# Row sums of the first layer's softmax: from VectorE's reductions to ScalarE's accumulated output

## The reference, cut to what is computed

```python
# x, ctx: 16 x 128 x 128, float32; 16 heads of 64
x = x + L0_xattn(keys=ctx, queries=layernorm(x), values=ctx)   # causal mask
x = x + L0_ffn(layernorm(x))         # width 352, inputs and weights quantised to blockwise FP4
x = x + L1_xattn(layernorm(x), ctx)  # two softmaxes: 77 text keys, 51 image keys, summed
x = x + L1_ffn(layernorm(x))         # 8 experts, top 2
# attention of the first layer
scores = q @ k.T / 8, masked to the lower triangle
attn = softmax(scores, axis=-1)      # exp(scores - row max) / row sum
out  = (attn @ v) @ Wo
```

## Time and profile before

| | us |
|---|---|
| median of 3 runs | 676.44 (675.97 to 677.09) |
| the profiled execution | 680.06 |
| its span, first to last instruction | 678.3 |
| first layer's attention, by the mask additions and the second layer's first maximum | 12.1 to 257.2 |
| busy: TensorE, VectorE, ScalarE, GpSimd | 619.6, 531.7, 440.1, 309.9 |

### The profile page before, as it was taken

The page is one execution under the profiler, slowest core; times in us unless marked ns, Lnnn a source line. Parts: engine busy times, 40 slices in busy tenths (PEclk is TensorE's granted clock), DMA queues, the critical chain, the costliest instruction groups (busy, mean ns, idle before and its releaser), DMA issues.

```text
span 678.3 us, 16643 instructions
## 1 busy us (share of the span) xinstructions
PE 619.6 (91%) x5833; PEld 569.8 (84%) x5833; DVE 531.7 (78%) x1446; ACT 440.1 (65%) x1125; POOL 309.9 (46%) x444
## 2 busy tenths in 40 slices
PE   5897999999999899999999999999999978989980
PEld 5786889988888799999989989889889967989980
DVE  5788897898988989888898896888565585656645
ACT  6776789887778786556665655565655364556750
POOL 3565344444444344454444442435245664466550
PEclk9899999999999999999999999999998898989995
DMA  9700000000000000336553050000000001112215
GB/s 225 247 2 1 1 2 1 2 1 2 1 1 1 3 17 1 126 88 140 102 121 83 2 156 1 2 1 2 2 13 21 28 29 49 54 53 69 75 48 190
DMA packets 49610, 33.34 MB, mean 49 GB/s; under 512 B 9508, under 2 KB 46088, under 8 KB 49528
## 3 DMA queue, kind: packets, MB, share of 16 engines
q1 hardware_dynamic: 47256, 27.61, 16.4%
q0 software_dynamic: 2272, 4.67, 2.1%
HBM read 17.64 MB, written 14.63 MB: 48 GB/s over the span
## 4 chain that ended last, share of the span: by engine, by line
PE 54%; issue 15%; DVE 15%; POOL 10%; ACT 4%; DMA 1%; another core or an unknown queue 0%; POOLq 0%; SPq 0%; DVEq 0%; ACTq 0%
PE ps_j L587 7%; PE ps_s L756 6%; PE ph L1705 5%; PE ps_h L809 5%; POOL probs L1521 5%; PE ps_t L794 5%; PE py L1716 4%; PE ps_h L826 4%; PE ps_j L367 4%; PE ps_j L369 3%; PE ps_j L368 3%; POOL xs_scratch L1632 3%; DVE scores L1246 3%; DVE neg_max L1253 2%; DVE sums L1261 2%
## 5 line engine op out<-in xcount | busy, mean ns | idle before, releaser
L1521 POOL TENSOR_TENSOR probs<-scores,rsums 128x308 f32<-128x308 f32 (+1 forms) x192 | 153.9, 816 | 215.2 <-DVE rsums L1266 213.4
L1261 DVE TENSOR_REDUCE sums<-scores 128x4 f32<-128x308 f32 (+1 forms) x192 | 90.7, 500 | 20.1 <-ACT scores L983 14.4
L953 ACT ACTIVATE probsT<-ps_t 128x512 f32<-128x512 f32 x128 | 76.1, 594 | 30.7 <-PE ps_t L794 29.8
L794 PE MATMUL ps_t<-ident,probs 128*128 128x128 f32 x512 | 79.8, 279 | 9.2 <-POOL probs L1521 8.5
L983 ACT ACTIVATE scores<-scores,neg_max 128x128 f32<-128x128 f32 x256 | 81.4, 393 | 1.7 <-DVE neg_max L1253 1.6
L756 PE MATMUL ps_s<-KT,QT 64*128 64x128 f32 x1024 | 75.3, 287 | 0.8 <-ACT KT L856 0.8
L809 PE MATMUL ps_h<-probsT,V 128*64 128x128 f32 x1024 | 70.9, 281 | 4.7 <-DVE x_sb L1026 4.7
L850 ACT ACTIVATE QT<-ps_j 128x512 f32<-128x512 f32 x64 | 38.3, 598 | 56.4 <-PE ps_j L369 56.0
L794 PEld LDWEIGHTS ps_t<-ident,probs 128*128 128x128 f32 x512 | 59.5, 142 | 13.5 <-POOL probs L1521 12.3
L756 PEld LDWEIGHTS ps_s<-KT,QT 64*128 64x128 f32 x1024 | 63.0, 189 | 8.9 <-issue 2.6
L826 PE MATMUL ps_h<-Wo,headsT 128*128 128x128 f32 x512 | 69.6, 280 | 1.0 <-ACT headsT L946 1.0
(11 more groups left out here) (238 smaller groups left out, 1615.8 us busy)
## 6 DMA issues: line engine op xcount, KB each, us to landing
xs_scratch<-xs SPq DMA_DIRECT2D x8, 1032.0 KB, 7.3
xt<-xs_scratch SPq DMA_DIRECT2D x39, 64.5 KB
w1b<-in_L_ffn_w_dram SPq DMA_DIRECT2D x1, 2048.0 KB, 8.2
big_raw<-in_L_ffn_w_dram SPq DMA_DIRECT2D x8, 256.0 KB, 4.5
ysum<-y_scratch SPq DMA_DIRECT2D x4, 512.0 KB, 5.3
Wo<-in_L_xattn_Wo_dram SPq DMA_DIRECT2D x2, 512.0 KB, 5.0
out_dram<-x_sb SPq DMA_DIRECT2D x4, 256.0 KB, 2.3
x_sb<-in_x_dram SPq DMA_DIRECT2D x3, 256.0 KB, 10.3
```

What stands on the lines that cost most here:

```text
L794: ins = nc.tensor.transpose(ps_pT[:, j * S:(j + 1) * S], probs[s % 2][:, j, :], ident[:, :])
L953: nc.scalar.activation(probsT[(s - 2) % 4][:, :, :].rearrange("p h s -> p (h s)"), ps_pT[:, :], ACT.Copy).then_inc(SS["pT_copied"], 1)
L1261: ins = nc.vector.tensor_reduce(sums[:, p4, i, :], scores[p4][:, :, k0:k1], AX_X, ALU.add)
L1521: ins = nc.gpsimd.tensor_tensor(probs[(s - 1) % 2][:, :, k0:k1], scores[r][:, :, k0:k1], rsums[:, r, i, :].rearrange("p (h a) -> p h a", a ...
```

## The change

ScalarE's four exponentials of a step in the first layer get an accumulated output: each writes the sum of its row into `sums`, the tile that VectorE's reduction wrote before. `exp_sums` returns at once for the first layer. `invert_sums` of the first layer waits for `exp_ready` in its place. The second layer is as before, but for `sum_ready`, which now counts from its first step. The trace shows an accumulated output of L864 as an instruction of its own, ACTIVATION_READ_ACCUMULATOR, behind the ACTIVATE.

```diff
--- before.py
+++ after.py
@@ -981,7 +981,8 @@
                         act.wait_ge(SS["max_ready"], n + 1)
                         for j in range(HB):
                             ins = nc.scalar.activation(scores[s % 4][:, j, :], scores[s % 4][:, j, :], ACT.Exp,
-                                                       bias=neg_max[:, s % 4, 0, j:j + 1])
+                                                       bias=neg_max[:, s % 4, 0, j:j + 1],
+                                                       accum_out=sums[:, s % 4, 0, j:j + 1])
                     else:
                         act.wait_ge(SS["shifted"], g * STEPS + s + 1)
                         ins = nc.scalar.activation(scores[s % 4][:, :, :], scores[s % 4][:, :, :], ACT.Exp)
@@ -1256,13 +1257,18 @@
 
             def exp_sums(n, p4, lay):
 
+                if lay == 0:
+                    return
                 dve.wait_ge(SS["exp_ready"], n)
                 for i, (k0, k1) in enumerate(SEGS[lay]):
                     ins = nc.vector.tensor_reduce(sums[:, p4, i, :], scores[p4][:, :, k0:k1], AX_X, ALU.add)
                 ins.then_inc(SS["sum_ready"], 1)
 
             def invert_sums(n, p4, lay):
-                dve.wait_ge(SS["sum_ready"], n)
+                if lay == 0:
+                    dve.wait_ge(SS["exp_ready"], n)
+                else:
+                    dve.wait_ge(SS["sum_ready"], n - GROUPS * STEPS)
                 nc.vector.reciprocal(rsums[:, p4, 0:len(SEGS[lay]), :],
                                      sums[:, p4, 0:len(SEGS[lay]), :]).then_inc(SS["sums_ready"], 1)
```

## The result

The changed kernel takes 668.12 us (median of 4 runs, 667.17 to 670.2), the kernel before 676.21 us beside it. The ratio is 0.9887, with a 95% interval from 0.9861 to 0.9913, so 8.1 us faster. The forecast was 666.7 with a range from 661.0 to 675.0. The profiled execution took 667.7 us, its span is 665.9.

A forecast was written before the change was run, and what follows sets the result against it. TensorE's instruction stream was taken to set the pace, with waits from VectorE's lateness on top. Terms -1.0 - 4.0 - 5.7 + 1.0 = -9.7 us, off the 676.44 us median, gave 666.7 us, range 661.0 to 675.0.

The forecast's parts named there:

- What bounds the kernel: First layer: TensorE's own instruction stream sets the pace, and waits caused by VectorE being late come on top.
- The price of a read: ScalarE, first layer: each of 256 accumulator reads costs 0.095 us, bounds 0 and 0.19, 24 us in all.
- 12.1 to 54: First layer's opening stretch in us: a little over half of TensorE's 1.8 us wait for probs goes, -1.0 us.
- the rounds: Three repeating ten-step stretches of 39.8 us, each with one FFN round: -1.9 us each, -5.7 in all.
- Rival C: First layer: TensorE's busy time hides room and ScalarE's occupancy sets the time; -24.6 us, 651.8 us, chance 0.05.
- 40 x 0.095 = 3.8 gives 35.6 of 39.9: One ten-step round: 40 exponentials' reads add 3.8 us to ScalarE, which is then busy 35.6 of 39.9 us.
- 98 to 137.7: First-layer stretch in us: nothing to win, ScalarE rises to 39.4 of 39.7 busy; +1.0 us, bounds 0 and +2.5.
- Rival A: First layer: later exponentials delay ScalarE's copies, TensorE waits for QT, KT or headsT; -3.8 us, 672.6 us, chance 0.18.
- The moved wait: VectorE's 14.4 us wait for exponentials moves from the sum to the reciprocal; costed at nothing, at most 0.38 a step.
- The signs: Expected in the new profile: VectorE 38 to 43 us less busy, ScalarE 24 more, silu_h and x_sb waits gone.
- rival B: First layer: ScalarE becomes the pace if a read costs 0.19 us; about +7 us, 683.7 us, chance 0.09.
- Rival D: Whole kernel: nothing measurable, the waits were TensorE's pipeline draining anyway; within 1.4 us of 676.44, chance 0.07.

The follow-up runs named there:

- the kernel with no sum: Against the kernel before: no row sum in the first layer, neither VectorE's reductions nor ScalarE's reads, reciprocal of a constant; 657.95 us, ratio 0.9743.
- the changed kernel's second trace: The changed kernel run and traced again without alteration, against the kernel before: 667.0 us, ratio 0.9866, first layer 238.5 us.
- before, sum later: The kernel before, with VectorE's sum in even steps of the first layer moved behind the x_sb update and first mask addition; 682.11 us, ratio 1.0032.
- the sums on both engines: The kernel before plus accumulated outputs on the exponentials, written to an unread spare tile, VectorE's reductions kept; 692.0 us, ratio 1.0235.
- even steps only: Against the kernel before: accumulated sums only in the first layer's even steps, VectorE still summing in odd steps; 675.8 us, ratio 0.9995.

## Why the prediction's total was right, and where its terms were not

The total fell where it was forecast, at 668.1 against 666.7. Its terms did not. Here they are beside the traces, as changes of the first layer's stages against the kernel before. The gain is that of the kernel with no sum. The cost is the changed kernel's second trace minus that one. The last column is the changed kernel in its first and second trace. The gain and the last column hold in steps 0 to 21 up to 1.5 us of the clock that the kernel before lost there. With the same VectorE work but a clock of 1.00 (before, sum later) steps 0 to 11 took 46.4 us, against 47.3.

| stage | forecast | gain | cost of reads | changed |
|---|---|---|---|---|
| steps 0 to 21 | -5.0 | -10.1 | +4.2 | -7.1, -5.9 |
| 22 to 33 | +1.0 | -0.3 | +1.8 | +1.5, +1.5 |
| 34 to 43 | -1.9 | -2.1 | +2.0 | 0.0, 0.0 |
| 44 to 53 | -1.9 | -3.0 | +1.9 | -1.1, -1.1 |
| 54 to 63 | -1.9 | -2.4 | +1.3 | -1.1, -1.1 |
| sum | -9.7 | -17.8 | +11.2 | -7.8, -6.6 |

**What bounds the kernel** was right. TensorE's stream sets the pace, VectorE's lateness lay on top, and without it TensorE hardly idles.

**The price of a read** was right. I took 0.095 us by the squares' rows, and the four exponentials grew from 1.17 to 1.54 us, 0.093 each. The exponentials' line alone was busy for 81.38 us of the first layer before, and is for 105.04 now, 23.7 more. ScalarE's busy time rose by only 16.4. I read that as more overlap of neighbours. Its copies run closer together now (185.87 to 186.35, 0.48 us, for an instruction of 0.59), and in the first layer it waits 23.1 us for TensorE, where it waited 39.2 before.

**The gain was too small by 7 us,** in two terms. For 12.1 to 54 I took 1.0 of the waits named for probs. No sum at all gave 5.0 up to step 11 and 5.1 from step 12 to 21. And in the rounds I counted the idle time that the waits name, 2.4 us at most. The kernel with no sum suggests that TensorE's busy time held waits too. In the first layer its busy time fell from 227.3 to 222.9 us with the same matmuls. So 13.4 of the 17.8 us were idle time, and 4.4 were shown as busy. I take these for waits too. Some can be the clock lost before, though the later sum, with 1.00 in the whole layer, was as busy (227.4). This bears on the rule of the Trainium skill that I weighed (Perfetto Trace Analysis, section Identifying the Most-Contended Engine). The section warns that matmul busy time is not a good measure of the distance to the limit. Here it hid 4.4 us of room. Weight loads, busy for 36.0 of 39.5 us in a stretch in which TensorE was never idle, show 3.5 us of room in that stretch alone, and no run here won it. Rival C, which went by it, is out: with the reads gone too, the time was 658, not 652.

**The cost was too small by 8 to 10 us.** The step that failed is "40 x 0.095 = 3.8 gives 35.6 of 39.9" taken as free room. I charged the reads only in 98 to 137.7, where ScalarE was nearly full. They cost 1.3 to 2.0 us a round all the same. Part of it shows as waits. With no sum TensorE waited 1.2 us for ScalarE's copies in the first layer, in the changed kernel's second trace 6.0, and 3.5 of the new 4.8 are for probsT. Another 5.1 us of the 11.2 lie in TensorE's busy time (222.9 to 228.0), where the profile names no wait. Here an engine that stands in the chain of every step cost time before it was full. Rival A described this in kind: the new waits for ScalarE's copies passed the 4 us that I gave as its sign, with 6.3, though most are for probsT and A named QT, KT and headsT. By that sign the forecast was wrong in its mechanism though its number held. Rival A stood at -3.8 in size, because it had the small gain as its base. The two errors, 7 us and 8 to 10, have opposite signs and nearly cancel. That the total came within 1.4 us is luck.

**The moved wait,** costed at nothing, gave a gain of 3.5 us of the first layer against the same wait at the old place. My reason for calling it free did not hold as such. I had half a microsecond left ahead of the reciprocal. In the changed kernel VectorE waits there, as its timeline shows:

```profile
184.87 0.69 DVE L1247 TENSOR_TENSOR scores<-ps_s,causal 128x512 f32<-128x512 f32 x1
186.01 0.18 DVE L1272 RECIPROCAL rsums<-sums 128x4 f32<-128x4 f32 x1 [0.45 <-ACT scores L983]
186.10 0.68 DVE L1247 TENSOR_TENSOR scores<-ps_s,causal 128x512 f32<-128x512 f32 x1
```

Relieved of its sums, VectorE gets there before ScalarE does. In the profile it waited 20.2 us at the reciprocal in all, where it had waited 14.4 at the sum. The shorter chain of a step (the reciprocal 0.30 us earlier) has no term of its own in the sum either. The two together were worth 8.7 us of the medians while the reductions' time stayed on VectorE; what part of that is clock isn't known.

**The signs.** VectorE is 38.1 us less busy, as forecast. The waits for silu_h and x_sb shrank to a third and did not vanish. Those for probs went. ScalarE is 16.4 us busier, not 24. The rounds took 39.8, 38.7 and 38.7 us, not 37.9. The stretch of steps 22 to 33 took 41.2, just past the 39.7 to 41 that was given. The second layer began at 249.4, not at 247.5. A start distance of over 0.46 us, the sign of rival B, was not seen (0.39). Rival D is out with the ratio.

## What to carry to other kernels

Moving a reduction from VectorE to the accumulated output of ScalarE's exponentials pays where VectorE's lateness shows in TensorE's waits. Here it was worth 17 to 18 us and gave back more than half of that, since ScalarE feeds TensorE in every step. Price such a move by two kernels, one with the old work taken out and one with the new work added beside the old. Here the busy time of the receiving engine understated the cost, and the named idle time of the bounding engine understated the gain. A third kernel, with the old work kept but out of the chain, tells its time from its place. Then try it on part of the steps. Here one half of them carried the whole gain.

## What the runs showed that I had not expected

The kernel that made TensorE wait more lost clock as well. With the sums on both engines TensorE was busy for 36.25 of 41.5 us, with waits between, and was granted 0.92 of 2.4 GHz there, so some of the stretch ran at 1.2 GHz. In the kernel before the same steps had 1.00. The rounds with 0.96 took 1.5 us longer than the round with 1.00. So a wait may cost more than its length. It isn't that kernel's alone: the kernel before had 0.96 in 12.1 to 54, and the one with even steps only had 0.95 and 0.96 in two stretches. A neighbouring round with like busy time (37.37 of 42.0) kept 1.00, so what decides isn't settled by these runs. When two traces differ by a microsecond or two, compare the granted clock of their stages first.
